# Two of four weight quarters turned by VectorE and memory instead of TensorE

## The reference

```python
x = x + _L0_cond_ref(x, ...)   # a state-space convolution over the 1024 columns
x = x + _L1_cond_ref(x, ...)   # x @ W.T + gated low-rank experts
x = x + _L2_cond_ref(x, ...)   # x @ W.T + a low-rank term chosen by label
x = x + _L3_cond_ref(x, ...)
...
# _L3_cond_ref
lora_delta = lora_B @ lora_A * (LORA_ALPHA / LORA_RANK)
cb = codebook / jnp.clip(jnp.max(jnp.abs(codebook)), 1e-08)
scale = jnp.exp(scale_log)
wg = (weight + lora_delta).reshape(O, I // GROUP, GROUP)
normalized = wg / scale
thresholds = (cb[:-1] + cb[1:]) * 0.5
idx = jnp.searchsorted(thresholds, normalized, side='left')
quantized = cb[idx]
w = quantized - normalized + normalized          # in this order
w_eff = (w * scale).reshape(O, I) + lora_delta
return x @ w_eff.T
```

## Time and profile before

| | us |
|---|---|
| median of three executions (lowest, highest) | 980.62 (980.4, 981.99) |
| the profiled execution, its time | 980.34 |
| the profiled execution, its span | 978.5 |
| TensorE (PE) busy | 968.8, 99% of the span |
| VectorE (DVE) busy | 835.1 |
| ScalarE (ACT) busy | 448.2 |
| GpSimd (POOL) busy | 276.0 |
| TensorE transposes of the four quarters (L990), 64 records | 9.61 |

### The profile page before, as it was taken

How to read it: one execution, slowest core, us unless ns; L and a number is a source line. 1 busy time by engine, 2 the same in 40 slices (tenths; PEclk the granted TensorE clock), 3 DMA queues, 4 the chain that set the end, 5 groups by cost and what they waited for, 6 DMA issues and landing times.

```text
span 978.5 us, 16678 instructions
## 1 busy us (share of the span) xinstructions
PE 968.8 (99%) x4773; PEld 781.7 (80%) x4773; DVE 835.1 (85%) x1663; ACT 448.2 (46%) x855; POOL 276.0 (28%) x346
## 2 busy tenths in 40 slices
PE   9999999999999999999999999999999999999998
PEld 5455459888888788888888888888888888888886
DVE  6899999989954888888988888888889888888863
ACT  3342526253565445545445444455454455454541
POOL 6600100945434332222322223322223322223100
PEclk9999999999999999999999999999999999999999
DMA  8924010102133455555554545655556545555321
GB/s 283 124 46 86 0 44 1 44 1 44 29 68 64 76 109 93 100 98 99 115 103 89 109 90 106 112 95 98 101 96 115 105 87 104 96 104 112 76 44 44
DMA packets 380589, 83.46 MB, mean 85 GB/s; under 512 B 353144, under 2 KB 373432, under 8 KB 380552
## 3 DMA queue, kind: packets, MB, share of 16 engines
q1 hardware_dynamic: 379544, 82.28, 44.2%
q10 hardware_dynamic: 1008, 0.76, 0.3%
HBM read 60.89 MB, written 20.71 MB: 83 GB/s over the span
## 4 chain that ended last, share of the span: by engine, by line
PE 96%; ACT 1%; ACTq 1%; issue 1%; DVE 1%; POOL 0%; DVEq 0%; POOLq 0%
PE bank L816 35%; PE bank L1033 12%; PE bank L971 10%; PE bank L803 7%; PE bank L782 5%; PE bank L837 5%; PE bank L793 4%; PE bank L771 4%; PE bank L807 4%; PE bank L949 3%; PE bank L982 2%; PE bank L843 2%; PE bank L827 1%; PE bank L990 1%; PE bank L915 1%
## 5 line engine op out<-in xcount | busy, mean ns | idle before, releaser
L816 PE MATMUL bank<-Mh,strips_r 128*128 128x512 f32 x1020 | 289.1, 395 | 0.0
L816 PEld LDWEIGHTS bank<-Mh,strips_r 128*128 128x128 f32 x1020 | 189.9, 188 | 40.9
L1109 ACT ACTIVATE SK<-ZZ 64x448 f32<-64x448 f32 x128 | 73.9, 577 | 215.1 <-DVE ZZ L1463 212.7
L577 POOL TENSOR_TENSOR Cl<-QC,Ch 128x256 fp32r<-128x256 f32 x32 | 39.0, 1218 | 450.0 <-ACT Ch L1091 450.0
L816 PE MATMUL bank<-Ml,strips_r 128*128 128x512 f32 x510 | 160.0, 395 | 0.0
L1463 DVE SCALAR_TENSOR_TENSOR ZZ<-ZZ,coef 128x192 f32<-128x192 f32 (+1 forms) x256 | 106.6, 456 | 10.1 <-DVE ZZ L1454 0.2
L816 PEld LDWEIGHTS bank<-Ml,strips_r 128*128 128x128 f32 x510 | 95.9, 188 | 22.6
L971 PE MATMUL bank<-E,A 128*128 128x512 f32 (+1 forms) x320 | 97.8, 466 | 0.0
L1454 DVE SCALAR_TENSOR_TENSOR ZZ<-ZZ,coef 128x384 f32<-128x384 f32 (+1 forms) x128 | 80.0, 625 | 12.8 <-DVE ZZ L1463 6.7
L971 PEld LDWEIGHTS bank<-E,A 128*128 128x128 f32 x320 | 51.0, 191 | 44.9 <-issue 44.3
L803 PE MATMUL bank<-Mh,strips_r 128*128 128x296 f32 x256 | 70.7, 299 | 0.0
(11 more groups left out here) (319 smaller groups left out, 1840.3 us busy)
## 6 DMA issues: line engine op xcount, KB each, us to landing
X<-in_x SPq DMA_DIRECT2D x256, 64.0 KB, 2.3
XT<-in_x SPq DMA_DIRECT2D x256, 64.0 KB, 2.2
out_x<-O SPq DMA_DIRECT2D x62, 256.0 KB, 3.2
toep<-kpad SPq DMA_DIRECT2D x128, 64.0 KB, 2.2
E<-in_L_cond_W SPq DMA_DIRECT2D x8, 512.0 KB, 7.0
vq<-in_L_cond_weight SPq DMA_DIRECT2D x8, 512.0 KB, 3.4
turned<-TB SPq DMA_DIRECT2D x29, 128.0 KB, 2.0
Bt<-turned SPq DMA_DIRECT2D x116, 32.0 KB, 2.1
```

Source lines behind the costliest of these rows:

```text
L816: pe.matmul(psO[nh][:, :], xs[:, c, :], ms[:, c, nh * BANK:(nh + 1) * BANK], start=(c == 0 and n == 0), stop=False)
L1109: act.activation(SK[ri * N:(ri + 1) * N, hh, :].rearrange("p (c b) -> p c b", b=B), ZZ[hh * N:(hh + 1) * N, :, ri, :], ACT.Copy).then_inc( ...
```

## The change

The quarters 0 and 1 (`TURNED = 2`) no longer pass through TensorE. VectorE, right behind the last operation of such a quarter, adds the identity to its diagonal block (128 x 128) and turns the tile in 32 x 32 squares into dq[q], whose content is used up; it does this for both tiles of the quarter (`q_turned`). SyncE stores dq[q] to memory in four DMAs, each square at its transposed place (`q_stored`), and loads the whole quarter from there into A3[q] (`a3_loaded`). ScalarE, before it may overwrite dq[0] or dq[1] with `delta` of quarter 2 or 3, waits for that store. TensorE's blocks `m` of the quarters 0 and 1 wait for the load. Two things come with it: VectorE's waits for `v_ready` and `quant_init` stand inside the branch that needs them and no longer ahead of all branches; and ScalarE's `state_columns` and GpSimd's first `expand_b` stand one entry earlier, behind the last entry of quarter 2.

```diff
@@ order
         for mt in range(MT):
-            order += [("lap", mt)] + stagings(0)[mt:mt + 1]
+            order.append(("lap", mt))
...
-                if q + 1 < QUARTERS and mt in (2, 4, 6, 7):
+                if TURNED <= q + 1 < QUARTERS and mt in (2, 4, 6, 7):
                     order.append(stagings(q + 1)[(2, 4, 6, 7).index(mt)])
@@ SyncE, behind next_w2(7)
-                for q in range(2, QUARTERS):
-                    next_w3(q)
+
+                def store_quarter(q):
+                    sp.wait_ge(q_turned, QT_TILES * (q + 1))
+
+                    for a in range(PARTS):
+                        dst = bass.AP(quarters.tensor, q * P * QCOLS + a * SPAN, [[QCOLS, SPAN], [P, QT_TILES * NC], [SPAN * QCOLS, PARTS], [1, SPAN]])
+                        sp.dma_start(dst, dq[q][a * SPAN:(a + 1) * SPAN, :, :].rearrange("p t k -> p (t k)").rearrange(
+                            "p (n k j) -> p n k j", k=PARTS, j=SPAN)).then_inc(q_stored, 16)
+
+                def load_quarter(q):
+                    sp.wait_ge(q_stored, 16 * PARTS * (q + 1))
+                    sp.dma_start(A3[q][:, :, :], quarters[q].rearrange("p (c o) -> p c o", c=NC)).then_inc(a3_loaded[q], 16)
+
+                store_quarter(0)
+                next_w3(2)
+                store_quarter(1)
+
+                sp.wait_ge(quant_done, 2)
+                load_quarter(0)
+                sp.wait_ge(lowrank_lo, 3)
+                load_quarter(1)
+                next_w3(3)
@@ GpSimd
-                        if j == ("m", LAST_Q, 0):
+                        if j == ("m", LAST_Q - 1, MT):
                             pool.wait_ge(cols_ready, 1)
                             expand_b(0, first=True)
@@ TensorE, ahead of the blocks of a quarter
-                        pe.wait_ge(stage_free, jobno[stagings(q)[-1]] + 1)
-                        pe.wait_ge(a3_ready, QT_TILES * (q + 1))
+                        if q < TURNED:
+                            pe.wait_ge(a3_loaded[q], 16)
+                        else:
+                            pe.wait_ge(stage_free, jobno[stagings(q)[-1]] + 1)
+                            pe.wait_ge(a3_ready, QT_TILES * (q + 1 - TURNED))
@@ ScalarE
                             act.wait_ge(quant_done, q - 1)
+                            act.wait_ge(q_stored, 16 * PARTS * (q - 1))
                         take(j, dq[q % 2][:, n // 2, n % 2 * BANK:(n % 2 + 1) * BANK], stage(j)[:, :])
...
-                        elif j == ("m", LAST_Q, 0):
+                        elif j == ("m", LAST_Q - 1, MT):
                             state_columns()
@@ VectorE
-                    dve.wait_ge(v_ready, q + 1)
-
-                    dve.wait_ge(quant_init, q + 1)
                     base = n_step[0]
...
                         with dve.If((n_kept & worth) > 0):
                             first = (n_kept >> (bit + 1)) << (bit + 1)
+                            dve.wait_ge(v_ready, q + 1)
+                            dve.wait_ge(quant_init, q + 1)
...
                     dve.tensor_tensor(qf, qf, df, ALU.add).then_inc(quant_done, 1)
+                    if q < TURNED:
+                        dve.wait_ge(quant_done, q + 1)
+                        for t in range(QT_TILES):
+                            d = qq[q][:, t, (q * QT_TILES + t) * P:(q * QT_TILES + t + 1) * P]
+                            step(dve.tensor_tensor(d, d, ident[:, :], ALU.add))
+
+                            dve.transpose(df.rearrange("p (c t k j) -> p t c k j", c=NC, k=PARTS, j=SPAN)[:, t],
+                                          qq[q][:, t, :].rearrange("p (c k r) -> p c k r", c=NC, k=PARTS)).then_inc(q_turned, 1)
```

More of the change, by code:

```diff
@@ L66, in resid_stack_kernel @@
     kpad = nc.dram_tensor("kpad", [H, 2, KP], F32, kind="Internal").ap()
+    TURNED = 2
+    quarters = nc.dram_tensor("quarters", [TURNED, P, 2 * L], F32, kind="Internal").ap()
     turned = nc.dram_tensor("turned", [P, HB * P], F32, kind="Internal").ap()
@@ L275, in resid_stack_kernel @@
         qt_full, qt_free, a3_ready = sem("qt_full"), sem("qt_free"), sem("a3_ready")
+        q_turned, q_stored, a3_loaded = sem("q_turned"), sem("q_stored"), [sem(f"a3_loaded{q}") for q in range(TURNED)]
         m_full, m_taken, m_lo, lowrank_hi, lowrank_lo = sem("m_full"), sem("m_taken"), sem("m_lo"), sem("lowrank_hi"), sem("lowrank_lo")
@@ L720, in _ @@
                             pool.wait_ge(m_lo, n)
-                            pool.wait_ge(a3_ready, QT_TILES * min(q + 2, QUARTERS))
+                            if q + 2 > TURNED:
+                                pool.wait_ge(a3_ready, QT_TILES * (min(q + 2, QUARTERS) - TURNED))
                         pool.tensor_tensor(lo, m32[rows, n % 2, :], hi.bitcast(F32), ALU.subtract).then_inc(m_lo, 1)
@@ L1316, in _ @@
                         if 4 <= mt < 4 + FIXED:
+                            act.wait_ge(q_turned, QT_TILES)
                             compare(2, mt - 4)
@@ L1326, in _ @@
                         q, n = which
-                        if (q, n) == (0, 0):
-                            act.wait_ge(quant_done, 2)
                         take(j, A3[q % 2][:, 2 * n:2 * n + 2, :], stage(j)[:, :].rearrange("p (t o) -> p t o", t=2))
@@ L1830, in _ @@
                 dve.wait_ge(quant_done, QUARTERS)
-                dve.wait_ge(stage_full, jobno[stagings(1)[-1]] + 1)
+                dve.wait_ge(q_turned, QT_TILES * TURNED)
+                dve.wait_ge(q_stored, 16 * PARTS * TURNED)
                 tb = [P, HH, MULT]
```

## The result

The changed kernel takes 985.15 us (median of six executions, 984.57 to 987.94), the kernel before 980.51 beside it on the same chip. The ratio is 1.0049, with a 95% interval of 1.0039 to 1.0059: slower. The profiled execution takes 984.57 us with a span of 982.8, so 4.2 and 4.3 us more than the one before.

The account below looks back on a forecast made before the run. TensorE, 96% of the chain, was taken to bound the kernel. Stagings removed -4.3, stall +6.5 and clock +1.6 gave +3.8 us: forecast 984.2 us, slower, range 981.0 to 989.8.

Parts of the forecast that it names:

- Stagings removed, -4.3: TensorE's eight stagings go: 2.5 us between the laps and 1.8 us within quarter 0's blocks, together -4.3 us.
- The turn at 142.8: VectorE ends quarter 1's turn at 142.8 us: 138.87, less 2.3 for moved waits, plus 6.2 for two turns.
- The store, 8.2 us: Quarter 1's four DMAs to memory, 8192 runs of 128 B, take 8.2 us; bounds 6.9 and 12.1.
- writing short runs costs twice: Rival, 18%: short writes cost double, store 12.1 us, stall 10.4, clock 1.6 to 2.1; +7.9 us, 988.2 us.
- Copy and handover 0.74: From the store's landing through ScalarE's dq copy to the first lap: 0.74 us, as before.
- The stall, +6.5: TensorE waits ahead of the laps; the first starts at 151.75 instead of 145.22 us, +6.5 us, nothing hidden.
- The clock, +1.6: TensorE's clock falls during its wait; some 4 us then run at the lower clock, +1.6 us, between 0 and 2.1.
- The sum: Whole kernel: -4.3 + 6.5 + 1.6 = +3.8 us.
- Cover and what is late next: Other loads, ScalarE and VectorE's quarter 3 (246 at worst, TensorE at 252) stay hidden; without the stall TensorE waits up to 2 us.
- short stall: Rival, 15%: best store rate and full 2.9 us of moved waits; first lap at 149.9, stall 4.7, 981.5 us.
- covered store: Rival, 6%: four DMAs through within 4 us of the turn, first lap by 147.5, clock holds; -2.0 us, 978.3 us.
- clock that holds: Rival, 15%: the stall ahead of the laps as forecast, but no clock fall; +2.2 us, 982.5 us.

Follow-up runs that it names:

- e10: Changed kernel with 8 extra, unread matmuls on TensorE ahead of the first lap; 984.65 us, ratio 1.0043.
- e4: Changed kernel with VectorE's waits on v_ready and quant_init put back ahead of the branches; 988.98 us, ratio 1.0082.
- e1: Changed kernel with quarter 3's first two delta entries behind the nine laps instead of ahead of them; 979.24 us, ratio 0.9986.
- e6: Changed kernel with the 32x32 squares exchanged by the load, so the store writes whole rows of 8 KB; 982.7 us, ratio 1.0024.
- e13: e6 with quarter 0's load held back until quarter 1's store has landed; each store reads 8 KB from 32 partitions; store 5.9 us.
- e7: Changed kernel with the stores in runs of 256 B, computing another result with the same work; store 8.3 us.
- e8: Changed kernel with the stores in runs of 512 B, computing another result with the same work; store 7.3 us.
- e11: e13 with each of the four stores reading 2 KB from all 128 partitions; store 4.7 us, 982.27 us in a single execution.
- e9: Changed kernel with quarter 3's first two delta entries behind the fourth lap; 978.1 us, ratio 0.9978.
- e2: Changed kernel with 16 extra, unread matmuls on TensorE ahead of the first lap; 989.16 us, ratio 1.0088.
- e5: Changed kernel with one turned quarter (TURNED = 1), quarter 1 staged by TensorE as before; 978.72 us, ratio 0.9984.
- e12: e9 with the turned quarters' identity added by GpSimd on A3a and A3b instead of by VectorE; 978.64 us, ratio 0.9986.

## Why the prediction was right, point by point

**Stagings removed, -4.3: right.** The laps with their stagings took 22.5 us before and 19.83 in e10, at the same clock: -2.7, predicted 2.5. Quarter 0's blocks run without the four pieces of 0.44 us: -1.8.

**The turn at 142.8: right in its terms, with luck in the last tenths**, 142.54. The addition took 0.29 and 0.25 us, the transpose 1.25, and the moved waits gave 2.3 us, as e4 shows from the other side. Ahead of the steps of quarters 0 and 2 VectorE's timeline has 0.68 and 0.64 us where it had 2.00 and 1.98: its sequencer now goes through the branches while the multiplication runs. The luck is in another row. One multiplication of quarter 0 took 3.03 us in the traced execution before, and 2.29 in that of the changed kernel:

```profile
35.39 3.03 DVE L1782 TENSOR_TENSOR vq<-vq,inv_scale 128x2048 f32<-128x2048 f32 x1
```

```profile
35.52 2.29 DVE L1809 TENSOR_TENSOR vq<-vq,inv_scale 128x2048 f32<-128x2048 f32 x1
```

It took 3.01 us in e1's execution, and there the turn of quarter 1 ended at 143.47. VectorE's idle times in the changed kernel:

```profile
38.50 1.53 DVE L1743 TENSOR_SCALAR step_t<-vq,steps 128x1024 f32<-128x1024 f32 x2 [0.68 <-DVE vq L1809]
...
147.86 0.81 DVE L1743 TENSOR_SCALAR step_t<-vq,steps 128x1024 f32<-128x1024 f32 x1 [0.64 <-DVE vq L1809]
```

**The store, 8.2 us: the term that was mis-sized**; it took 9.2. The number came from a cost for each short run, taken from loads: their mean rate with nothing added for the direction, or their best rate times 1.2. The best rate was not there to be had. The store's windows of 137 to 150 GB/s are 1070 to 1170 runs of 128 B a us, as the loads had at their mean, against 1560 in their best window. Part of the extra 1.0 us can be the load into A3a, which was issued 3.0 us before the store's end: by my estimate the store's 1.05 MB, at the 144 GB/s of the four windows from 144 to 148, would have been through at 151.1, 0.7 us earlier. I had that load queue behind the store. No run holds it back with runs of 128 B; with rows of 8 KB (e6, e13) that was worth 0.2 us. The range for the store held, but e7 and e8 show that the time does not go with the number of runs: four times fewer runs saved 1.9 of the 9.2 us. e13 and e11 show the second cause, 32 partitions in each DMA, that I had not considered at all. My rival that writing short runs costs twice is gone: it had 12.1 us. The Trainium skill, "DMA: Bandwidth & Descriptors", Specifications, puts the border at 512 B and speaks of a read-modify-write below it; here the step from 256 B to 512 B is about as big as the one below it (1.0 and 0.9 us). The full set is 128 B 9.2 us, 256 B 8.3, 512 B 7.3, 8 KB 6.1 (5.9 with the load held back), and 4.7 from 128 partitions.

**Copy and handover 0.74: right**, 0.82 (151.79 to 152.61).

**The stall, +6.5: it was 7.4**, by the store's extra 1.0.

**The clock, +1.6: close, but by two errors that offset each other.** It fell, 3.7 us after TensorE's last matmul, and cost 1.35 us. I had 4 us of laps at the lower level, losing 0.4 of that time. The low stretch reached only 2.8 us into the laps, and they lost half of it. Both my numbers came from the start of the trace, and that start shows no low clock: the column of the granted clock reads 1.00 in the windows in which the weight loads took 231 ns. What made them slow there stays open. One of these windows of the kernel before, with the matmuls of L889 alone (third number from the end):

```profile
3.50:4.50 1.00, 1.00 (x6) 1.00 (x6) 1.00 0.53 131
```

**The sum.** The measured sum is -2.7 - 1.8 + 7.4 + 1.35 = +4.25 us, and the span grew by 4.3.

**Cover and what is late next: right in what it lists, but it leaves one out.** No wait stands at A3a, A3b or quarter 0's `delta`. VectorE ended quarter 3 at 244.70 (I had 246 at worst) and TensorE came at 252.46. The prediction said that without the stall TensorE would come at 243.8 and wait for VectorE up to some 2 us; in e9 it waits 1.26, until 244.86. There TensorE was 4.5 us ahead of the kernel before when quarter 2's blocks began (233.13 against 237.62) and 3.1 at staging (3,3) (244.92 against 247.98); its median is 2.4 us lower. The rows of the changed kernel for this place, VectorE's last operation on quarter 3 and TensorE's staging:

```profile
242.41 2.29 DVE L1851 TENSOR_TENSOR quant<-quant,dq 128x2048 f32<-128x2048 f32 x1
```

```profile
252.46 0.44 PE bank L1015 x4
```

What is left out is quarter 0's turn, which makes VectorE, and so ScalarE's comparisons of quarter 1, later. They stand ahead of the copies (`tabs`) for which TensorE waits at quarter 2's second `delta` half. Before the change ScalarE was idle for 1.29 us between them; in the changed kernel nothing of it is left. ScalarE's first copy before, then the comparisons and that copy after:

```profile
101.68 0.45 ACT L1277 ACTIVATE tabs<-bank 64x64 f32<-64x64 f32 x2 [1.29 <-PE bank L936]
```

```profile
97.83 3.90 ACT L1270 ACTIVATE above<-vq,fixed_tau 128x2048 uint8<-128x2048 f32 x2 [3.10 <-DVE vq L1809]
101.71 0.45 ACT L1306 ACTIVATE tabs<-bank 64x64 f32<-64x64 f32 x2
```

TensorE waits 0.27 us there in both traces. But wherever VectorE is later than this, TensorE waits longer: 1.16 us in e1, 1.4 in e7, 1.8 in e4. In the changed kernel the stall behind it would hide such a wait; in e1 it costs 0.9 us.

**The rivals.** The short stall, the covered store and the clock that holds did not occur. The nearest to the covered store is e11: its store took 4.7 us and landed at 147.31, and the clock still fell. The prediction drew the border to a faster kernel at a store end of 146.8 us. Its own terms (-4.3, and 1.6 for the clock) put it at 147.2, and e11 came out even at the start of the tiles.

## What to carry to other kernels

A buffer that gets a second use keeps its next writer waiting, and what stands behind that writer in an in-order list waits too. Look for the list's order first: four laps put ahead of the waiting copy (e9) turned 4.6 us of loss into a gain of 2.4, where the fastest store that I found (e11) only came out even at the start of the tiles.

For a transfer that someone waits for, count the partitions of each DMA as well as the length of its runs, and put the scattered side where there is time: here the load had 20 us of laps to hide in, and the store had nothing.

## What the runs showed of the hardware that I had not expected

The clock's fall can outlive the wait that caused it. With TensorE's wait cut from 7.7 us to 4.5 (e6) the low stretch lay from 147.3 to 154.1, and the laps lost 2.2 us instead of 1.4. In e11, after 3.2 us without work, the clock fell at 148.7, when the laps had already been running for 0.6 us, and came back at 152.2. In the kernels whose longest wait here was 2.3 us or less (e1, e2, e5, e9, e10, e12) it was never low at this place.

That is no safe length, though. In e11 and in e4's traced execution the clock fell a second time in the tiles, at 333.1 and at 341.0, 1.6 us after the end of a wait of 1.3 us, for 3.4 us each. The same wait stands in all fourteen traces (1.31 us before the change, 1.32 after), and in the other twelve no low stretch follows it. Executions of one kernel differ by up to 3.4 us, and some of the slower ones have a lower mean clock: the changed kernel's slowest, 987.94 us, has 0.992 where the other five have 0.996. A second low stretch would explain that, but only the two traces show one.

What a low stretch costs could be read four times: the laps lost 1.35 us of 2.8 in the changed kernel, 2.2 of 4.5 in e6, 1.6 of 3.4 in e11 and 2.3 of 4.8 in e4, against the 19.83 us that e10's laps took. It is half each time.

Which of VectorE and GpSimd starts first can decide how long both take. In eleven traces GpSimd's operation on `E` starts after VectorE's multiplication at about 35.5, and VectorE's takes 2.29 us and GpSimd's 4.4 to 5.4. In three (the kernel before, e1, e7) GpSimd's starts first, by 0.15 to 0.3 us, and VectorE's takes 3.0 us and GpSimd's 2.8 to 2.9. GpSimd waits for a load there, so the landing of a DMA at 35 us moved the turn of a quarter at 142 us by 0.7. Before and after the change:

```profile
35.24 2.77 POOL L679 TENSOR_SCALAR E<-E 128x1024 f32<-128x1024 f32 x1 [0.96 <-DMA E<-in_L_cond_B]
```

```profile
36.26 4.67 POOL L703 TENSOR_SCALAR E<-E 128x1024 f32<-128x1024 f32 x1 [1.85 <-DMA E<-in_L_cond_B]
```

VectorE's four operations on 128 x 2048 behind quarter 2's steps took 9.51 us in the changed kernel, where GpSimd started its subtractions at 176.73, and 14.22 us in e9, where it started at 167.95. In both kernels they had started at 168.5. Most of it came back in the two operations behind them, which took 3.39 and 3.81 us in the changed kernel and 1.63 each in e9: of 4.7 us, 1.0 is left by the multiplication with the scale (188.44 against 189.46).
